# Linear attention: head sums per chunk, epsilon and reciprocal on 128x128, and their product placed behind the first value projection

## The reference, cut to what matters

```python
q = phi((x @ W_Q.T).reshape(b, t, H, DK))      # phi(u) = elu(u) + 1
k = phi((x @ W_K.T).reshape(b, t, H, DK))
v = (x @ W_V.T).reshape(b, t, H, DK)
gamma = sigmoid(decay_log)                     # one per head
# for every token, in order:
S = gamma * S + outer(k_t, v_t)                # 64x64 per head
z = gamma * z + k_t                            # 64 per head
y_t = (S^T q_t) / (sum(z * q_t) + EPS)         # sum over the 64 features of the head
gate = sigmoid(x @ W_g_w.T + W_g_b)
out = (y * gate) @ W_O.T
```

## Time and profile before

| what | value |
|---|---|
| median of three runs | 1889.74 us |
| span of the profiled execution | 1886.0 us |
| TensorE matmul busy (PE) | 1843.9 us, 98% |
| weight load busy (PEld) | 1541.7 us, 82% |
| VectorE busy | 1395.0 us, 74% |
| ScalarE busy | 881.7 us, 47% |
| GpSimd busy | 589.6 us, 31% |
| granted TensorE clock | 0.999 |

### The profile page before, as it was taken

The page is one execution under the profiler, slowest core; times in us unless marked ns, Lnnn a source line. Parts: engine busy times, 40 slices in busy tenths (PEclk is TensorE's granted clock), DMA queues, the critical chain, the costliest instruction groups (busy, mean ns, idle before and its releaser), DMA issues.

```text
span 1886.0 us, 36455 instructions
## 1 busy us (share of the span) xinstructions
PE 1843.9 (98%) x12481; PEld 1541.7 (82%) x12481; DVE 1395.0 (74%) x2679; ACT 881.7 (47%) x1717; POOL 589.6 (31%) x526
## 2 busy tenths in 40 slices
PE   8999999999999999999999999999999998999998
PEld 7888888888888888878787888788878877888887
DVE  6566566556668888777777878787878788888885
ACT  6656656665554444453333333333333332444443
POOL 5313203311332222233433333333333334522211
PEclk9999999999999999999999999999999999999999
DMA  7100000000022122120000000000000001222322
GB/s 246 43 1 0 0 0 0 0 0 0 13 54 54 29 33 32 29 62 13 13 12 12 11 11 11 11 11 11 11 11 11 12 12 20 38 62 62 65 55 58
DMA packets 230630, 53.19 MB, mean 28 GB/s; under 512 B 209696, under 2 KB 228768, under 8 KB 230176
## 3 DMA queue, kind: packets, MB, share of 16 engines
q1 hardware_dynamic: 229296, 49.53, 13.0%
q10 hardware_dynamic: 1264, 2.76, 0.4%
HBM read 18.69 MB, written 8.39 MB: 14 GB/s over the span
## 4 chain that ended last, share of the span: by engine, by line
PE 74%; DVE 9%; issue 6%; POOL 4%; SPq 2%; ACT 2%; DMA 1%; DVEq 0%; ACTq 0%; POOLq 0%
PE PS L1203 16%; PE PS L1212 9%; PE PS L322 8%; PE PS L331 7%; PE PS L861 7%; PE PS L832 6%; PE PS L850 3%; PE PS L1732 3%; PE PS L1706 3%; PE PS L1668 3%; SPq L270 2%; PE PS L1711 2%; PE PS L1721 2%; PE PS L872 2%; DVE lin_zq L1504 2%
## 5 line engine op out<-in xcount | busy, mean ns | idle before, releaser
L322 PE MATMUL PS<-ln_xh,lin_w 128*128 128x512 f32 x768 | 249.9, 394 | 9.2 <-POOL ln_xl L280 5.4
L1135 ACT ACTIVATE ff_silu<-PS 128x512 f32<-128x512 f32 x192 | 114.4, 597 | 232.9 <-PE PS L1203 204.5
L1170 DVE SCALAR_TENSOR_TENSOR ff_h<-PS,ff_silu 128x512 f32<-128x512 f32 x192 | 131.2, 684 | 107.7 <-PE PS L1203 94.1
L322 PEld LDWEIGHTS PS<-ln_xh,lin_w 128*128 128x128 f32 x768 | 144.3, 188 | 47.6 <-DVE lin_kT L1487 8.6
L568 POOL TENSOR_TENSOR qk<-qk,swapped 64x128 f32<-64x128 f32 (+2 forms) x96 | 96.9, 1009 | 240.2 <-DVE swapped L712 234.4
L1154 DVE TENSOR_TENSOR ff_h_lo<-ff_h,ff_h_hi 128x512 fp32r<-128x512 f32 x192 | 165.1, 860 | 0.4
L861 PE MATMUL PS<-probT,v_a 128*128 128x128 f32 x1152 | 153.3, 278 | 0.0
L861 PEld LDWEIGHTS PS<-probT,v_a 128*128 128x128 f32 x1152 | 139.5, 192 | 14.3 <-ACT probT L632 7.4
L322 PE MATMUL PS<-ln_xl,lin_w 128*128 128x512 f32 x384 | 150.2, 391 | 0.0
L832 PE MATMUL PS<-qk 128*128 128x512 f32 (+3 forms) x384 | 145.2, 489 | 1.0 <-POOL qk L568 0.9
L722 DVE TENSOR_REDUCE neg_max<-PS 128x1 f32<-128x256 f32 (+7 forms) x128 | 95.6, 752 | 62.3 <-PE PS L835 60.9
(11 more groups left out here) (190 smaller groups left out, 5354.2 us busy)
## 6 DMA issues: line engine op xcount, KB each, us to landing
ff_raw<-ln_xn SPq DMA_DIRECT2D x464, 32.0 KB, 2.0
ln_xl<-ln_xn SPq DMA_DIRECT2D x288, 32.0 KB, 2.0
out_x<-X SPq DMA_DIRECT2D x15, 512.0 KB, 2.9
X<-in_x SPq DMA_DIRECT2D x7, 1024.0 KB, 5.5
stage<-in_w_lin SPq DMA_DIRECT2D x1, 2048.0 KB, 8.1
stage<-in_w_gate SPq DMA_DIRECT2D x2, 768.0 KB, 7.4
stage<-in_w_up SPq DMA_DIRECT2D x2, 768.0 KB, 8.8
stage<-in_w_down SPq DMA_DIRECT2D x2, 768.0 KB, 10.2
```

The lines of the kernel that those rows point to most:

```text
L322: last = nc.tensor.matmul(out, w, x, start=n == 0, stop=n == len(terms) - 1)
L1135: nc.scalar.activation(silu[:, f % NB_GU, :], PS[:, f % NB_GU, :], ACT.Silu, scale=W_SCALE).then_inc(silu_done.sem, 1)
L1170: nc.vector.scalar_tensor_tensor(h[:, f % 2, :], PS[:, NB_GU + f % NB_GU, :], W_SCALE, silu[:, f % NB_GU, :], ALU.mult, ALU.mult).then_inc ...
```

## The change

The head sums of chunk c (of 4) are put on rows of their own: rows 4c to 4c+3 of each 16 for the first head, rows 16+4c to 16+4c+3 for the second. For that head_sum gets 12 more columns (it becomes 128x44, zeros but for four columns of ones in each half of the partitions), and a 128x32 window of it, shifted by 4 columns per chunk, is the weight. The four chunks accumulate into the same 128 columns of PSUM bank 7, so that the result is 128x128, with all four chunks one under the other. Epsilon, doubling and reciprocal work on 128x128. The spread takes for each chunk the row where its sum lies and writes 128 columns of the same bank as before. The product stands behind item 12, the first value projection, and not behind the keys ahead of it.

```diff
-        den = z[0]
+        den = zq[:, 0, 0:P]
-        head_sum, z_last = sb("head_sum", [P, SUM]), sb("z_last", [P, NP])
+        head_sum, z_last = sb("head_sum", [P, SUM + 3 * DUP]), sb("z_last", [P, NP])
+        def sum_rows(r, c):
+            at = (UT * r + c) * DUP
+            return slice(at, at + DUP)
...
+            nc.gpsimd.memset(head_sum[:], 0.0).then_inc(zeroed, 1)
             for r in range(2):
-                for c in range(2):
-                    pool.wait_ge(zeroed, 1 + 2 * r + c)
-                    nc.gpsimd.memset(head_sum[r * DK:(r + 1) * DK, c * SUM // 2:(c + 1) * SUM // 2],
-                                     1.0 if r == c else 0.0).then_inc(zeroed, 1)
-            pool.wait_ge(zeroed, 5)
+                pool.wait_ge(zeroed, 2 + r)
+                at = 3 * DUP + sum_rows(r, 0).start
+                nc.gpsimd.memset(head_sum[r * DK:(r + 1) * DK, at:at + DUP], 1.0).then_inc(zeroed, 1)
+            pool.wait_ge(zeroed, NZERO)
...
-                nc.vector.tensor_scalar(den, PS[:, DEN_BANK, :], DEN_EPS, 2.0, ALU.add, ALU.mult).then_inc(den_done.sem, 1)
+                nc.vector.tensor_scalar(den, PS[:, DEN_BANK, 0:P], DEN_EPS, 2.0, ALU.add, ALU.mult).then_inc(den_done.sem, 1)
...
-                for j in range(NP):
-                    last = nc.tensor.matmul(PS[j * SUM:(j + 1) * SUM, DEN_BANK, :], head_sum[:], z[j], start=True, stop=True)
+                for c in range(UT):
+                    for j in range(NP):
+                        last = nc.tensor.matmul(PS[j * SUM:(j + 1) * SUM, DEN_BANK, 0:P], head_sum[:, (3 - c) * DUP:(3 - c) * DUP + SUM],
+                                                z[j][:, c * P:(c + 1) * P], start=c == 0, stop=c == UT - 1)
...
-                for j in range(NP):
-                    rows = slice(j * SUM, (j + 1) * SUM)
-                    for r in range(2):
-                        row = j * SUM + r * SUM // 2
-                        last = nc.tensor.matmul(PS[r * DK:(r + 1) * DK, SPREAD_BANK[j], :],
-                                                ident[rows, row:row + 1].to_broadcast([SUM, DK]), den[rows, :],
-                                                start=True, stop=True)
+                for c in range(UT):
+                    for j in range(NP):
+                        rows = slice(j * SUM, (j + 1) * SUM)
+                        for r in range(2):
+                            row = j * SUM + sum_rows(r, c).start
+                            last = nc.tensor.matmul(PS[r * DK:(r + 1) * DK, SPREAD_BANK[j], c * P:(c + 1) * P],
+                                                    ident[rows, row:row + 1].to_broadcast([SUM, DK]), den[rows, :],
+                                                    start=True, stop=True)
...
                             if first and half == 0:
-                                pe.wait_ge(zeroed, 5)
+                                pe.wait_ge(zeroed, NZERO)
+                        if it == 3 * NP:
                             denominators(b, half)
```

More of the change, by code:

```diff
@@ L54 @@
 SUM = P // NP
+DUP = SUM // (2 * UT)
 DEN_EPS = 1e-6
@@ L1304, in linear_attention_phase @@
         NITEM = 3 * NP + UT
+        NZERO = 4
+        def sum_rows(r, c):
+            at = (UT * r + c) * DUP
+            return slice(at, at + DUP)
         const_loaded, prep_wo = signals.const_loaded, signals.prep_wo
@@ L1585, in turn @@
                         dve.wait_ge(masked, 1)
-                        dve.wait_ge(zeroed, 5)
+                        dve.wait_ge(zeroed, NZERO)
                     decayed_scores(b, c0, 0)
```

## The result

| | before | after |
|---|---|---|
| median, 9 runs each side by side | 1889.74 us | 1895.07 us |
| span of the profiled execution | 1886.0 us | 1893.3 us |

The ratio is 1.0034 [1.0025, 1.0043]: the change makes the kernel slower by 0.34%. The forecast was 1887.1 us, 2.65 us faster; the time lies in its range (1879.5 to 1897), the direction is wrong.

The account below looks back on a forecast made before the run. TensorE, with matmuls busy 98% of the span, was taken as the bound. Terms -7.05 - 2.9 + 1.3 + 6.0 = -2.65 us took 1889.74 to 1887.1 us, range 1879.5 to 1897.

Parts of the forecast that it names:

- the loop's code: TensorE's loop branch: the grown body no longer stays loaded, each of five taken branches refetches, +1.2 us each, +6.0 us.
- rival 3: Loop branch: refetch uncovered or longer, 3.2 us five times, and clock loss behind it; +16 for +6, 1897 us; chance 0.08.
- The moved product, -7.05: Head-sum product behind the first value projection: TensorE's wait for the last z tile goes in 15 halves, -7.05 us.
- First half, -2.9: First half of the first sequence: a projection fills part of TensorE's gap, clock stays at 2.4 GHz; -2.9 us.
- Shorter matmuls, +1.3: Product and spread as more, shorter matmuls: +0.03 and +0.05 us a half, 16 halves, +1.3 us.
- Rival 2: Product and spread: every short matmul pays its own start, 64 ns a record; +62 us net, 1951.8 us; chance 0.07.
- VectorE, 0: Shorter inverse: frees 45 us of VectorE and starts DMAs earlier, but TensorE's split-input wait stays; 0 us.
- rival 4: Split input before a half's first projection: earlier DMAs also remove the 5.4 us wait; 1881.7 us; chance 0.08.
- Rival 1: TensorE's loop: the grown body still fits, so no refetch and no +6.0; 1881.1 us; chance 0.27.

Follow-up runs that it names:

- e3: The whole change with TensorE's program written out for all eight sequences, no loop; 1883.89 us, 0.996 of the kernel before.
- e1: The kernel before with only the product moved behind the first value projection, 512 columns kept; 1886.27 us, ratio 0.9981.
- e6: The whole change with two sums of 256 columns in place of four of 128; 1882.47 us, 0.9959 of the kernel before.
- e7: The kernel before with the product moved and epsilon and reciprocal on only 128 of 512 columns, the rest not inverted; 1879.1 us, ratio 0.9942.
- e2: The changed kernel with the product back in its old place, so chunk sums alone; 1903.52 us, 1.0082 of the kernel before.
- e9: The kernel before with TensorE's program written out, no loop; 1892.8 us, ratio 1.0017.
- e5: The kernel before with 96 more idle instructions in TensorE's loop body, 3 behind each projection; 1908.12 us, ratio 1.0094.
- e4: The kernel before with 288 more idle instructions in TensorE's loop body, 9 behind each projection; 1916.77 us, ratio 1.0141.
- e11: The kernel before with 64 more idle instructions in TensorE's loop body, 2 behind each projection; 1908.56 us, ratio 1.0101.

## Why the prediction was wrong, step by step

**The failed step** is "+1.2 us, five times, +6.0 us" of the loop's code. Its mechanism was right: the body outgrew what stays loaded, 42 packets came in five passes ("some 40 more" was forecast), and the branch took 3.5 to 4.1 us ("near 3.4"). Its size was not. The five passes of after exceed the 96.30 of e3, the same work without a branch, by 3.75 + 3.22 + 3.15 + 3.13 + 1.62 = 14.9 us. So the term should have been +14.9 and not +6.0, and with it the sum turns from faster to slower. Two parts:

- *The stall is uncovered more than I took.* From the last output matmul to the first projection it is 3.13, 2.62, 2.56, 2.59 and 2.57 us, 1.00 in before: 8.5 us more, and not 6.0. Against the 0.93 of e3 it is 8.8 of the 14.9. I worked with 3.45 us from a single branch; the real ones are longer, and TensorE resumes another 0.26 us behind the branch's end (1107.13 + 3.61 = 1110.74, then 1111.00).
- *The clock.* The other 6.1 us stand in the four passes with a granted clock near 0.6, 1.5 in each. I had "clock loss behind the gap" only in rival 3, at a chance of 0.08, though the earlier trace rows show it: 0.57 behind an idle 3.44 us. I argued from 2.83 busy us in 4 that shorter idle time leaves the clock alone. In the first half that held in this trace (1.00 behind 2.03 us idle) and in e1's, but not in those of e3, e6 and e7; behind the branch 2.3 to 2.9 us idle cost it in four of five. I had one row of a lost clock behind a stall of TensorE, and should have carried its price for the five new stalls in the likeliest case's own range.

Rival 3 stood at +16, 1897 us; measured were 14.9 and 1895.07. It named both parts, and it was the right case. That its number is near is luck: its 16 is five branches with nothing covered (3.2 us each) and nothing for the clock, where 8.8 us of stall and 6.1 of clock were measured. That the measured time lies in the stated range rests on this number, too.

**The moved product, -7.05**: right. All 15 waits are gone, no row is idle before L1686 but in the first half, and it runs behind the first value projection. A pass of e7 is 0.90 us shorter than one of before, where two of the 15 waits are 0.94.

**First half, -2.9**: right in this execution, 8.24 to 5.34 us with the clock at 1.00, but in part by luck: in e3, e6 and e7 the scores lie 12.0 to 12.1 us apart and not 10.51, so they won 1.4 us, which is what the prediction gave for a clock that falls all the same.

**Shorter matmuls, +1.3**: nearly right: the product +0.01 and the spread +0.10 us, 0.11 x 16 = +1.8. Rival 2 is out: 64 records in 1.14 us are 18 ns each, not 64. The tiles of one round share their start. By an estimate from the 81 ns per matmul of "TensorE: Matmul & The Clock Gate", section "Back-to-back issue gap" of the Trainium skill the spread would take 5.2 us. The trace doesn't agree where eight small tiles run together: it has 1.14.

**VectorE, 0**: right for what it was asked of, wrong as a general statement. In the old place it is worth nothing (e2: its passes are 2 us longer, 1.8 of stall and 0.2 of shorter matmuls, with no gain); but most of what the move wins exists only with it. I took its 7.05 and the first half's 2.9 as the move's own, 9.95 in all; e1 shows the move alone at 3.9, e7 at 11 with the relief. The sum of the prediction wasn't touched, since it priced both together. The DMAs of ln_xl start 1.7 us earlier against the next scores (0.34 behind L1675, 2.01 in the earlier trace rows), where 1.9 was forecast, and the wait for the split input falls from 5.4 in 9 to 4.6 in 7 in e3: rival 4 is out, with 0.8 of its 5.4.

**Together**: without the loop's effect -7.05 - 2.9 + 1.8 = -8.2 us; e3 measures -6.2 against before and -8.9 against e9. With it -8.2 + 14.9 = +6.7. The traces of before and after say the same where the change acts: 729.9 to 739.6 us from the first spread to the last, and 2.9 less ahead of that, +6.7. The medians say +5.3, the spans +7.3.

**Rival 1**, that the body fits, is the world of e6: it gave 1881.1 and that kernel takes 1882.5.

The Trainium skill, "Runtime: NRT & Kernel Launch", section "Instruction fetch mechanics", states that a taken branch whose target isn't in the current window of two pages has to fetch it before the engine goes on. The traces agree on the stall and on blocks of 16 KiB (42 packets of 0.69 MB are 16.4 KB each). They do not agree on a window of two: a body of six packets came with one packet over five branches in before. The section's store of 128 KiB fits where the step lies, if a body that touches 7 blocks stays beside one fetched ahead. That reading is an estimate from the page and the step between 32 and 64 instructions. What is shown is the step and that the place of the body shifts it.

**Open**: why the same idle time costs the clock in one pass or execution and not in the next (four passes of five here, none in e2's trace behind 2.5 to 2.6 us idle). Of the 1 us by which e5's passes are longer than those of after at the same branch, 0.7 is that e5 keeps the old place (97.0 against 96.3); the rest is not explained, but in four of its five passes TensorE waits a second time for the split input, 0.25 to 0.61 us, which after does not.

## What to carry to other kernels

Before code is added inside a loop, read the code queue and the loop's branch: one packet and 208 ns mean that the body is loaded, and how far the step is can be tried with a few idle instructions. If the body is near it, prefer the version with fewer instructions (two sums of 256 columns kept nearly all of the gain), or shift the body, and look again after each edit ahead of the loop. Price a stall of TensorE of 2 us or more with and without the clock behind it, as one execution may not show it; and ask of each pair of edits whether one pays only in the presence of the other.

## What was not expected of the hardware

- 64 more instructions in a loop cost 19 us where 32 cost nothing, 1% of the kernel; the same 96 cost 18 us or, with the body shifted, at most 4.
- A taken branch into code that isn't loaded takes TensorE 3.4 to 4.1 us (after, e2, e4, e5, e11), and the body comes anew in every pass: 42 packets in five.
- The clock behind the same idle time differs from execution to execution: behind 2.0 us in the first half it stayed at 1.00 in after and e1 and fell in e3, e6 and e7; behind 3.44 us it fell in before and stayed in e2. Where it fell it cost some 1.5 us.
- Matmuls of 128 columns on eight tiles of 32x64 run at 18 ns a record, on four of 128x32 at 1.01 us for 32.
- The reciprocal takes 3.35, 1.75 and 0.95 us for 512, 256 and 128 columns: 6.3 ns a column and 0.15 us.
